# Conditioned residual maps on Trainium2: pairs 8 to 61 loaded two at a time, four channels side by side in a partition

## The reference, cut to what matters

```
x: (128, 128, 2048)   W0: (16, 128, 128)   W1: (32, 128, 128)   b1: (32, 1, 128)
x = x + einsum('bct,bcd->bdt', x, W0[i0])
x = x + einsum('bct,bcd->bdt', x, W1[i1]) + transpose(b1[i1], (0, 2, 1))
```

## Time and profile before

| | |
|---|---|
| median of 3 runs | 638.94 us |
| the profiled execution's own time | 638.89 us |
| its span (first to last instruction) | 637.1 us |
| PE busy | 546.6 us, 86% of the span, 2334 MATMULs |
| PE weight loads busy | 237.4 us |
| DVE, ACT, POOL busy | 331.6, 324.5, 128.2 us |
| DMA | 271.73 MB in 19297 packets, 427 GB/s over the span |
| TensorE clock granted, mean | 0.994 of full |

### The profile page before, as it was taken

How to read it: one execution, slowest core, us unless ns; L and a number is a source line. 1 busy time by engine, 2 the same in 40 slices (tenths; PEclk the granted TensorE clock), 3 DMA queues, 4 the chain that set the end, 5 groups by cost and what they waited for, 6 DMA issues and landing times.

```text
span 637.1 us, 6039 instructions
## 1 busy us (share of the span) xinstructions
PE 546.6 (86%) x2334; PEld 237.4 (37%) x2334; DVE 331.6 (52%) x270; ACT 324.5 (51%) x326; POOL 128.2 (20%) x274
## 2 busy tenths in 40 slices
PE   1899999999989888898898988988889889888894
PEld 1344444444334333343343333433433333333331
DVE  1266666666555455544554455445554555455542
ACT  0366666666455455544554455445554455455542
POOL 2322222222122121221211212212112122121101
PEclk9999999999999999999999999999999999999997
DMA  8999999999999999999999999999999999999998
GB/s 358 434 408 433 428 428 431 433 432 428 431 432 432 432 428 432 430 433 431 428 433 433 430 431 427 433 433 431 430 428 434 432 431 429 428 434 433 430 430 350
DMA packets 19297, 271.73 MB, mean 427 GB/s; under 512 B 2565, under 2 KB 2598, under 8 KB 2662
## 3 DMA queue, kind: packets, MB, share of 16 engines
q1 hardware_dynamic: 9504, 137.37, 50.6%
q10 hardware_dynamic: 9398, 132.81, 48.7%
q0 software_dynamic: 384, 1.44, 0.6%
HBM read 137.40 MB, written 134.22 MB: 426 GB/s over the span
## 4 chain that ended last, share of the span: by engine, by line
DMA 65%; PE 30%; DVE 3%; ACT 0%; issue 0%; ACTq 0%; DVEq 0%
DMA out_dram<-xt 40%; PE acc L229 25%; DMA xt<-in_x_dram 23%; PE acc L224 4%; DMA cond_rep<-in_conds_dram 2%; DVE xt L308 1%; DVE xt L307 1%; PE acc L278 1%; ACT L343 0%; ACT spare L372 0%; PE acc L216 0%; ACT both L343 0%; ACTq L325 0%; DVE biasT_even L293 0%; PE acc L218 0%
## 5 line engine op out<-in xcount | busy, mean ns | idle before, releaser
L229 PE MATMUL acc<-xt,both 64*128 64x512 f32 x2048 | 471.9, 603 | 67.7 <-DMA xt<-in_x_dram 65.5
L346 ACT ACTIVATE xt<-acc,bias_of 64x1024 f32<-64x1024 f32 x252 | 279.2, 1108 | 275.8 <-PE acc L229 273.4
L229 PEld LDWEIGHTS acc<-xt,both 64*128 64x128 f32 x2048 | 189.5, 187 | 318.3 <-issue 213.9
L307 DVE TENSOR_SCALAR xt<-acc,bias_of 64x1024 f32<-64x1024 f32 x126 | 160.8, 1276 | 273.0 <-PE acc L229 273.0
L308 DVE TENSOR_SCALAR xt<-acc,bias_of 64x1024 f32<-64x1024 f32 x126 | 162.5, 1290 | 1.8
L179 POOL TENSOR_TENSOR map0T<-w0T_sb,ident 128x128 f32<-128x128 f32 x128 | 65.6, 512 | 466.1 <-PE acc L224 454.2
L224 PE MATMUL acc<-map,map0T 128*128 128x256 f32 x260 | 74.4, 409 | 0.4 <-DVE bias_away L302 0.4
L193 POOL TENSOR_TENSOR map<-w_sb,ident 128x128 f32<-128x128 f32 x126 | 64.5, 512 | 0.0
L224 PEld LDWEIGHTS acc<-map,map0T 128*128 128x128 f32 x260 | 44.5, 191 | 52.5 <-issue 36.9
L343 ACT ACTIVATE both<-acc 128x512 f32<-128x512 f32 x64 | 38.2, 597 | 0.7
L343 ACT ACT_TABLE_LOAD x1 | 1.3, 1283 | 18.7 <-PE acc L224 18.7
(11 more groups left out here) (28 smaller groups left out, 12.2 us busy)
## 6 DMA issues: line engine op xcount, KB each, us to landing
xt<-in_x_dram SPq DMA_DIRECT2D x64, 2048.0 KB, 24.5
out_dram<-xt ACTq DMA_DIRECT2D x63, 2048.0 KB, 42.9
w_sb<-in_w_dram SPq DMA_DIRECT2D x1, 2048.0 KB, 9.5
w0T_sb<-in_w0T_dram SPq DMA_DIRECT2D x1, 1024.0 KB, 5.0
out_dram<-last POOLq DMA_DIRECT2D x2, 512.0 KB, 8.2
out_dram<-last POOLq DMA_DIRECT2D x2, 192.0 KB, 7.6
out_dram<-last ACTq DMA_DIRECT2D x1, 256.0 KB
out_dram<-spare ACTq DMA_DIRECT2D x2, 128.0 KB
```

What stands on the lines that cost most here:

```text
L229: return nc.tensor.matmul(acc[:, j * CHUNK:(j + 1) * CHUNK], both[k * HC:(k + 1) * HC, buf, u, k, :], xt[k * HC:(k + 1) * HC, slot, u * T ...
L307: nc.vector.tensor_scalar(to[0:HC, a:a + HALF], acc0[0:HC, a:a + HALF], bias[0:HC, :], None, ALU.add)
L346: return nc.scalar.activation(to[HC:C, v * T + a:v * T + a + HALF], acc1[v * HC:(v + 1) * HC, a:a + HALF], ACT.Identity, bias=bias[v * HC: ...
```

## The change

Pairs 0 to 7, 62 and 63 stay as they are. Pairs 8 to 61 are taken two together, as 27 quads of four samples. The tables `units` lists the pairs and quads in order.

- **Load.** One DMA of 4096 KB brings a quad into two neighbouring slots (L171 of the new kernel). Partition 32 s + i holds channels 4 i to 4 i + 3 of sample s, side by side: 32 KB, contiguous in HBM. It waits until both pairs that held the slots are stored.
- **Products.** `quad_term` multiplies 32 partitions (one sample, k = 0 to 3) with the map of one of the four channels (u) over 512 steps. Four samples go to four different banks: k = 0 and 2 to `acc0`, k = 1 and 3 to `acc1`. A chunk of 512 steps is sixteen terms, and a quad is four chunks, so a quad has 64 terms where two pairs had 32. The low and high half of the accumulators are now one chunk each.
- **Combining.** A quad's maps take sixteen matmuls of 32 weight columns and 128 moving columns, each into 32 partitions of one bank, before the last four terms of the second chunk. It waits for the maps and for the emptying of the first chunk (`lo_out`), since it writes into a bank of that chunk.
- **Emptying.** DVE and ACT each make four pieces of 64 by 512 per chunk, sixteen per quad, where they had four of 64 by 1024 per pair. Both wait for both accumulators.
- **Stores.** They keep their layout and size, two per quad, both issued once the quad's last chunk is emptied.
- POOL's additions keep their number and size; for quads they write `map0T` in four groups of channels.

```diff
+    x_quads = x.rearrange("(g s) (i u) t -> g (s i) (u t)", s=4, u=4)
+    units = [(q, 1) for q in range(SLOTS)] + [(q, 2) for q in range(SLOTS, PAIRS - 2, 2)] + [(PAIRS - 2, 1), (PAIRS - 1, 1)]
...
-            for q in range(PAIRS):
+            for q, pairs in units:
                 slot = q % SLOTS
                 if q >= SLOTS:
-                    sp.wait_ge(stored[slot], LOAD * (q // SLOTS))
-                sp.dma_start(xt[:, slot, :], x_pairs[q, :, :]).then_inc(x_loaded[slot], LOAD)
+                    for p in range(pairs):
+                        sp.wait_ge(stored[slot + p], LOAD * (q // SLOTS))
+                if pairs == 2:
+                    sp.dma_start(xt_quad[:, slot // 2, :], x_quads[q // 2, :, :]).then_inc(quad_loaded[slot // 2], LOAD)
+                else:
+                    sp.dma_start(xt[:, slot, :], x_pairs[q, :, :]).then_inc(x_loaded[slot], LOAD)
...
+            def combine(pairs, buf, at):
+
+                if pairs == 2:
+                    for u in range(4):
+                        for k in range(4):
+                            last = nc.tensor.matmul(acc1[k * QC:(k + 1) * QC, at + u * C:at + (u + 1) * C],
+                                                    map0T_quad[:, buf, u, k, :], map1[:, buf, k, :, :], start=True, stop=True)
...
+            def quad_term(k, u, buf, slot, j):
+
+                at = j % 2 * HALF + k // 2 * CHUNK
+                return nc.tensor.matmul((acc0, acc1)[k % 2][:, at:at + CHUNK], both_quad[k * QC:(k + 1) * QC, buf, u, :],
+                                        xt_quad[k * QC:(k + 1) * QC, slot // 2, u * T + j * CHUNK:u * T + (j + 1) * CHUNK],
+                                        start=u == 0, stop=u == 3)
...
+            def quad(slot, buf, outs, loads, next_slot, next_pairs, next_count):
+                prev = (slot - 1) % SLOTS
+                pe.wait_ge(quad_loaded[slot // 2], loads)
+                for u in range(4):
+                    quad_term(0, u, buf, slot, 0)
+                    quad_term(1, u, buf, slot, 0)
+                    done0 = quad_term(2, u, buf, slot, 0)
+                    done1 = quad_term(3, u, buf, slot, 0)
+                done0.then_inc(lo_done0, 1)
+                done1.then_inc(lo_done1, 1)
+                pe.wait_ge(hi_out[prev], outs)
+                for u in range(4):
+                    if u == 3:
+
+                        pe.wait_ge(maps_ready[next_slot], next_count)
+                        pe.wait_ge(lo_out[slot], outs)
+                        combine(next_pairs, 1 - buf, CB_QUAD)
+                    quad_term(0, u, buf, slot, 1)
+                    quad_term(1, u, buf, slot, 1)
+                    done0 = quad_term(2, u, buf, slot, 1)
+                    done1 = quad_term(3, u, buf, slot, 1)
+                done0.then_inc(hi_done0, 1)
+                done1.then_inc(hi_done1, 1)
+
+                pe.wait_ge(both_ready[next_slot], next_count)
...
+                pe.wait_ge(hi_out[slot], outs)
+                for u in range(4):
+                    quad_term(0, u, buf, slot, 3)
+                    quad_term(1, u, buf, slot, 3)
+                    done0 = quad_term(2, u, buf, slot, 3)
+                    if u == 3:
+                        pe.wait_ge(lo_out[slot + 1], outs)
+                    done1 = quad_term(3, u, buf, slot, 3)
...
+            def even_quad_out(q, j):
+
+                for p in range(2):
+                    at = j % 2 * HALF + p * CHUNK
+                    bias = bias_of[:, 2 * (q + p):2 * (q + p) + 1]
+                    nc.vector.tensor_scalar(xt[0:HC, q % SLOTS + p, j * CHUNK:(j + 1) * CHUNK],
+                                            acc0[0:HC, at:at + CHUNK], bias[0:HC, :], None, ALU.add)
+                    out = nc.vector.tensor_scalar(xt[0:HC, q % SLOTS + p, T + j * CHUNK:T + (j + 1) * CHUNK],
+                                                  acc0[HC:C, at:at + CHUNK], bias[HC:C, :], None, ALU.add)
+                return out
```

More of the change, by code:

```diff
@@ L127, in conditioned_residual_kernel @@
         x_loaded = [sem(f"x_loaded{q}") for q in range(SLOTS)]
+        quad_loaded = [sem(f"quad_loaded{g}") for g in range(SLOTS // 2)]
         stored = [sem(f"stored{q}") for q in range(SLOTS)]
@@ L231, in term, with pair @@
                                         start=u == 0, stop=u == 1)
-            def pair(slot, outs, next_count, loads):
-                buf = slot % 2
-                prev, next = (slot - 1) % SLOTS, (slot + 1) % SLOTS
+            def quad_term(k, u, buf, slot, j):
[3 more added lines that the diff above has]
+                                        start=u == 0, stop=u == 3)
+            def pair(slot, buf, outs, loads, next_slot, next_pairs, next_count):
+                prev = (slot - 1) % SLOTS
                 pe.wait_ge(x_loaded[slot], loads)
@@ L249, in pair @@
                 pe.wait_ge(hi_out[prev], outs)
-                combine(next)
+                if next_pairs:
+                    combine(next_pairs, 1 - buf, CB)
                 term(acc0, 0, 0, buf, slot, 2)
@@ L266, in _ @@
             pe.wait_ge(maps_ready[0], 1)
-            combine(0)
+            combine(1, 0, CB)
             pe.wait_ge(both_ready[0], 1)
-            with pe.Fori(1, TURNS + 1) as now:
-                for s in range(SLOTS):
-                    pair(s, now * 2, now + 1 if s == SLOTS - 1 else now, now * LOAD)
+            for s in range(SLOTS - 1):
+                pair(s, s % 2, 2, LOAD, s + 1, 1, 1)
+            pair(SLOTS - 1, 1, 2, LOAD, 0, 2, 2)
+            quad(0, 0, 4, LOAD, 2, 2, 2)
+            quad(2, 1, 4, LOAD, 4, 2, 2)
+            with pe.Fori(1, TURNS - 1) as now:
+                quad(4, 0, now * 2 + 2, now * LOAD, 6, 2, now + 1)
+                quad(6, 1, now * 2 + 2, now * LOAD, 0, 2, now + 2)
+                quad(0, 0, now * 2 + 4, now * LOAD + LOAD, 2, 2, now + 2)
+                quad(2, 1, now * 2 + 4, now * LOAD + LOAD, 4, 2, now + 2)
+            quad(4, 0, 2 * TURNS, (TURNS - 1) * LOAD, SLOTS - 2, 1, TURNS)
+            pair(SLOTS - 2, 1, 2 * TURNS, 2 * LOAD, SLOTS - 1, 1, 2)
+            pair(SLOTS - 1, 0, 2 * TURNS, 2 * LOAD, 0, 0, 0)
             pe.wait_ge(lo_out[SLOTS - 1], 2 * TURNS)
+            pe.wait_ge(both_ready[0], TURNS + 1)
             for j in range(T // CHUNK):
@@ L347, in odd_out, with odd_quad_out @@
                                             ACT.Identity, bias=bias[v * HC:(v + 1) * HC, :])
-            copy_maps(0)
-            for q in range(PAIRS):
-                to, bias = xt[:, q % SLOTS, :], bias_of[:, 2 * q + 1:2 * q + 2]
+            def odd_quad_out(q, j):
+                for p in range(2):
+                    at = j % 2 * HALF + p * CHUNK
+                    bias = bias_of[:, 2 * (q + p) + 1:2 * (q + p) + 2]
+                    for v in range(2):
+                        out = nc.scalar.activation(xt[HC:C, q % SLOTS + p, v * T + j * CHUNK:v * T + (j + 1) * CHUNK],
+                                                   acc1[v * HC:(v + 1) * HC, at:at + CHUNK], ACT.Identity, bias=bias[v * HC:(v + 1) * HC, :])
+                return out
+            copy_maps(0, CB)
+            for n, (q, pairs) in enumerate(units):
+                slot = q % SLOTS
+                if pairs == 2:
+                    for p in range(2):
+                        act.wait_ge(lo_done0, q + p + 1)
+                        act.wait_ge(lo_done1, q + p + 1)
+                        odd_quad_out(q, 2 * p).then_inc(lo_out[slot + p], 1)
+                        if p == 0:
+                            copy_maps(n + 1, CB_QUAD)
+                        act.wait_ge(hi_done0, q + p + 1)
+                        act.wait_ge(hi_done1, q + p + 1)
+                        odd_quad_out(q, 2 * p + 1).then_inc(hi_out[slot + p], 1)
+                    act.wait_ge(hi_out[slot + 1], 2 * (q // SLOTS + 1) + (2 if slot + 1 == SLOTS - 1 else 0))
+                    for p in range(2):
+                        act.dma_start(out_pairs[q + p, :, :], xt[:, slot + p, :]).then_inc(stored[slot + p], LOAD)
+                    continue
+                to, bias = xt[:, slot, :], bias_of[:, 2 * q + 1:2 * q + 2]
                 if q == PAIRS - 1:
```

100 lines of the change are left out of this document (67 added, 33 removed).

## The result

The changed kernel takes **661.15 us** (median of 4 runs, 657.45 to 663.11) where the kernel before took 639.13 on the same chip: ratio 1.034, 95% interval 1.029 to 1.039. The forecast was 637.6 us, and the range ended at 641.5. The profiled execution took 657.45 us for a span of 655.5, 18.4 us longer than the span before. Later runs of the same kernel on another chip went from 658 to 681 us, beside 638 to 640 of the kernel before: it has a spread that the old one lacks. Ratios leave out runs that are over 1.5% above the fastest of their kernel; medians are of all runs.

What follows compares the result with a forecast made beforehand. The prediction took the DMA engines' moving of the bytes as the bound. Savings of 0.9 us for packets, 0.1 for completions and 0.3 at the end made 1.3 us off 638.94, so 637.6 us, range 635.5 to 641.5.

Steps and rivals of the forecast that it cites:

- The queues stay filled: Load and store queues: 59.5 us remain per slot for a load and two stores that need 19.5 us.
- loads get two thirds: DMA at the end: 32 KB load packets alternate with 16 KB store packets, so quads land sooner; 0.3 us less.
- four slots: Rival at the slots: four are too few, both queues run empty 0.2 us per quad, 643 us; chance 0.05.
- Packets: DMA engines: 216 fewer packets on each at 4 ns save 0.9 us, between 0 and 2.2.
- longer packets: Rival in the loads: longer packets are 1% slower per byte, 640 to 641.5 us; chance 0.06.
- The end: DMA as the last pieces trickle out: 0.3 us won back, between 0 and 1.5, its pieces not touched.
- PE: PE per quad: terms 14.1, combining 1.1, waits 1.0, sum 16.2 us, below 19.65, so it costs nothing.
- The clock: PE after a 3.4 us gap before each quad: a fallen clock costs 2.2 us, nothing on the end.
- Both PE rivals: PE as bound: row quarters not fully overlapping, 748 us, chance 0.07; column quarters in turn, 716 us, chance 0.05.
- four signs: Signs of being wrong: middle DMA share below 0.98, no PE load waits, a round above 0.52 us, falling 431 GB/s.
- signs of being right: Fewer packets, DMA share 1.0, PE idle 3 us per quad, 0.43 us rounds, combining 1.1, last load before 24 us.

Runs made afterwards that it cites:

- half_loads: The changed kernel with each quad loaded by two DMAs of 16 KB packets, each issued once its own slot is stored: 652.2 us, ratio 1.020.
- more_matmuls: The kernel before with eight more one-column matmuls in each combining, their results unread: 641.3 us, ratio 1.004.
- three_queues: The changed kernel with the second store of each quad issued by GpSimd on its own queue: 652.9 us, ratio 1.020.
- change_again: The changed kernel unchanged, run again in the same rounds as three_queues: 672.7 us (658.1 to 680.9).
- split_rows: The changed kernel with each quad load split into two DMAs of 64 partitions, issued together: 847.0 us, ratio 1.325.

## Why the prediction was wrong

**The failing step** is "The queues stay filled", which was argued from 59.5 us for a load and two stores that need 19.5. It took the queueing time of two queues in sum. The text itself gave the missing half, "loads get two thirds", but drew only a better end from it: quads land sooner. That share came true, 66 to 68% of the bytes while both queues work. A load that is through in 20.2 us, issued every 20.2 us, leaves nothing behind it in its queue. The waiting moved to the stores, whose 38 to 40 us hold the slots and so the next load. The rival of **four slots** named the place and had 0.2 us per quad at 0.05; the middle lost 13.1 / 27 = 0.5 us per quad, and not by idle engines, as it said, but mostly by slow packets at a share of 1.00.

**Packets**: the fixed part was of the right size, two packets of 611 ns against 1213, and 216 x 9 ns = 1.9 us lay within the bounds of 0 to 2.2; the restart costs seven times that. The rival of **longer packets** is refuted: with equal packets on both queues 32 KB cost 1233 ns, 9 more than before.

**The end** was forecast to give back 0.3 us, "since the end's pieces are not touched". It costs 5.2. What was left out is that PE starts a quad late and has 42 us of work from the last quad's load on, so that it still has 21.5 us when the very last load lands, where it had 15.4; 6.0 us are shown for the end by quads in half_loads.

**Number of instructions**: no term, since PE's time alone was counted. In half_loads it is some 5 us, estimated from the records of landings and more_matmuls: 13 us remain there when the queue is cured; 6.0 for the end and 5.4 for this nearly make them up. In the change itself middle and end already make up its 18.4 us, and its last loads land complete within 2 us of their last but one part, so there this cost can't be told apart; how it would add up stays open.

**PE** came as forecast: a round of four 0.43 us; combining 1.08 for 1.1; a quad 17.2 us for 16.2. The 1.0 too little is in the waits for emptying, since ACT's piece takes 681 ns, not 597, and DVE's 743 and 756, not 714. The Trainium skill (TensorE: Matmul & The Clock Gate, Measured speedup vs the span model) has 3.07x for four row tiles, from which the prediction estimated 0.56 us for a round; the trace, with 0.43, does not agree. **The clock**: a gap of 4.09 us makes the next 56 MATMULs 8.31 instead of 6.29 us, 2.0 for the 2.2 forecast, and from 322.1 to 324.5 us, behind that gap, the granted clock is 0.50, its level of 1.2 GHz. It stays hidden: 17.2 + 2.0 is below 20.2, and three_queues reaches 428 GB/s with a mean clock of 0.94, little above the 0.92 of the change. **Both PE rivals** are refuted.

Of the four signs that the prediction said would show it wrong, three would have misled: the DMA share did not fall below 0.98 in the middle, PE kept its waits for loads, and a round stayed under 0.52 us. The fourth, falling GB/s, was the one. Most of its signs of being right came true as well: q1 has 9504 - 5616 = 3888 packets fewer, which is 3456 + 432, and the last load lands 29.5 us before the end, earlier than the 24. None of them says how long a load packet takes.

The profiled execution is the fastest of its four; what the median has beyond it, 661.15 - 657.45 = 3.7 us, may be more of the slow packets: the profiled execution of change_again, on another chip, has 1312 ns per 32 KB for a span of 657.7. No trace of the slower three shows it.

## What to carry to other kernels

Before making one stream's packets larger, ask which share of the DMA engines each queue will then have, and whether the faster one still has a transfer waiting behind the one in work; compare a transfer's time from issue to landing with the time between two issues. Make the packets of both directions larger together (which here still cost 1.1%), or leave them. And read GB/s beside the DMA share: a full share with falling bytes says that packets take longer, here behind a queue's restart, in split_rows all through a load; a stretch at a sixteenth of the rate is one engine left alone.

No version tried beats the kernel before.

## What was unexpected of the hardware

- A DMA queue that has run dry restarts slowly: packets of 16 KB took about 800 ns over their 611, those of 32 KB 598 over 1213, 1 to 2 us after the issue, less from 2 us on, and it was gone 7 to 8 us after the issue. The share counts it as busy.
- Quad loads as two DMAs over 64 partitions each: 2010 ns per 32 KB, 310 GB/s in all.
- One DMA engine falls behind, by an estimate from three kernels about 1 ns per executed instruction.
- ACT's second store issue behind a first takes longer: the two took between 0.8 and 1.9 us in the changed kernel, where one took 0.34 us in the kernel before.
